# First batch of a fused attention and expert kernel: where the group norm's chain and the next batch's row norm stand in the order by hand

## The reference, cut to what matters

```
def _L0_attn_ref(x, Wqkv_w, Wqkv_b, gn_w, gn_b, out_w, out_b):
    qkv = x @ Wqkv_w.T + Wqkv_b
    a = jnp.einsum('bthd,bshd->bhts', q, k)
    ctx = jnp.einsum('bhts,bshd->bthd', a, v)
    g = ctx.transpose(0, 2, 3, 1)
    mean = g.mean(axis=(2, 3), keepdims=True)
    var = ((g - mean) ** 2).mean(axis=(2, 3), keepdims=True)
    gh = (g - mean) * jax.lax.rsqrt(var + EPS)
    gh = gh * gn_w.reshape(H, Dh, 1) + gn_b.reshape(H, Dh, 1)
    return ctx @ out_w.T + out_b
...
x = x + _layernorm(_L0_attn_ref(_layernorm(x, axis=-1), ...), axis=-1)
x = x + _layernorm(_L0_ffn_ref(_layernorm(x, axis=-1), ...), axis=-1)
```

## Time and profile before

| | us |
|---|---|
| median of 3 runs | 855.06 |
| the 3 runs | 855.31, 852.76, 855.06 |
| the profiled execution | 854.16 |
| its span in the trace | 852.4 |
| PE busy in the span | 784.7 (92%) |
| DVE busy | 583.6 (68%) |
| ACT busy | 487.4 (57%) |
| POOL busy | 290.2 (34%) |

### The profile page before, as it was taken

One profiled execution on the slowest core, in us unless ns is written; L12 is line 12 of the kernel. 1 busy time (PEld: TensorE's weight loads), 2 busy tenths in 40 slices (PEclk: granted clock), 3 DMA queues, 4 the chain that ended last, 5 costly groups with the idle time before them and its releaser, 6 DMA issues.

```text
span 852.4 us, 21050 instructions
## 1 busy us (share of the span) xinstructions
PE 784.7 (92%) x6573; PEld 643.7 (76%) x6582; DVE 583.6 (68%) x1588; ACT 487.4 (57%) x1073; POOL 290.2 (34%) x316
## 2 busy tenths in 40 slices
PE   6989999999999998666999999999999999999991
PEld 2547777777777776444788888888888888888880
DVE  5758989898989888894787444555555555555553
ACT  4355848575766675421566555565656565656562
POOL 3011010101010000072265555555555555555542
PEclk9999999999999999997999999999999999999996
DMA  4114444343526161502244555646464646474733
GB/s 192 50 50 156 119 153 126 141 145 118 162 93 191 64 188 43 149 9 68 48 66 77 100 76 72 125 74 146 75 148 74 145 72 143 71 147 71 145 44 95
DMA packets 102692, 90.10 MB, mean 106 GB/s; under 512 B 63761, under 2 KB 94225, under 8 KB 101457
## 3 DMA queue, kind: packets, MB, share of 16 engines
q1 hardware_dynamic: 87648, 68.45, 27.5%
q0 software_dynamic: 14976, 20.78, 17.1%
HBM read 48.70 MB, written 27.39 MB: 89 GB/s over the span
## 4 chain that ended last, share of the span: by engine, by line
PE 72%; DVE 16%; ACT 5%; issue 4%; POOL 2%; DMA 1%; SPq 0%; ACTq 0%; DVEq 0%; POOLq 0%
PE ps L918 41%; PE ps L933 19%; PE ps L1002 4%; PE ps L1034 3%; DVE wgu L1289 3%; PE ps L996 2%; DVE hf L1229 2%; ACT wgu L778 2%; DVE wdn L1289 1%; DVE st L1405 1%; DVE wdn L1538 1%; PE ps L963 1%; DVE st L1209 1%; DVE hT L1239 1%; PE ps L1005 1%
## 5 line engine op out<-in xcount | busy, mean ns | idle before, releaser
L918 PE MATMUL ps<-xhl,wgu 128*128 128x256 f16 x3102 | 387.6, 275 | 12.3 <-DMA xhl<-attw 6.7
L918 PEld LDWEIGHTS ps<-xhl,wgu 128*128 (+1 forms) x3102 | 304.5, 99 | 56.0 <-issue 8.6
L1229 DVE SCALAR_TENSOR_TENSOR hf<-ps,sc,silu 128x256 f32<-128x256 f32 x330 | 159.6, 484 | 188.8 <-ACT silu L730 163.4
L730 ACT ACTIVATE silu<-ps,sc 128x256 f32<-128x256 f32 x275 | 130.4, 474 | 236.2 <-PE ps L918 236.1
L933 PE MATMUL ps<-wdn,hT 128*128 (+1 forms) x1870 | 252.8, 273 | 9.6 <-DVE hT L1239 7.2
L933 PEld LDWEIGHTS ps<-wdn,hT 128*128 128x128 f16 x1870 | 181.9, 98 | 35.1 <-DVE hT L1239 6.3
L673 POOL DMA_INDIRECT acc_d<-ysb,gst x78 | 128.8, 1651 | 44.5 <-POOL gst L669 30.9
L606 POOL TENSOR_TENSOR rstd<-ve,mhalf 128x4 f32<-128x4 f32 (+1 forms) x32 | 30.7, 960 | 294.6 <-DVE ve L1214 272.9
L1239 DVE TENSOR_TENSOR hT<-hf,hT 128x256 f16<-128x256 f32 x275 | 114.7, 417 | 1.7
L744 ACT CAST hT<-hf 128x256 f16<-128x256 f32 x275 | 109.7, 399 | 8.8 <-DVE hf L1229 7.1
L662 POOL DMA_INDIRECT attw<-xn_d,gst x78 | 80.1, 1027 | 44.5 <-POOL gst L658 32.6
(11 more groups left out here) (245 smaller groups left out, 768.0 us busy)
## 6 DMA issues: line engine op xcount, KB each, us to landing
wgu<-in_gu SPq DMA_DIRECT2D x8, 1408.0 KB, 6.4
att<-in_x SPq DMA_DIRECT2D x16, 512.0 KB, 5.5
wdn<-in_dn SPq DMA_DIRECT2D x8, 768.0 KB, 8.1
x_d<-att SPq DMA_DIRECT2D x8, 512.0 KB, 2.9
xn_d<-wgu SPq DMA_DIRECT2D x8, 512.0 KB, 3.3
acc_d<-ysb SPq DMA_DIRECT2D x16, 256.0 KB, 3.3
att<-x_d SPq DMA_DIRECT2D x8, 512.0 KB, 4.9
att<-acc_d SPq DMA_DIRECT2D x7, 512.0 KB
```

Source lines behind the costliest of these rows:

```text
L730: a.activation(silu[:, c % 2 * TW:(c % 2 + 1) * TW], gu_ps[c % 2][:, 0:TW], ACT.Silu, scale=scale_of(slot, 0)).then_inc(silu_made, 1)
L918: ins = te.matmul(o, slot_gu(slot, hw, k, j), x(hx, k), start=(n == 0), stop=(n == len(TERMS) - 1))
L1229: v.scalar_tensor_tensor(out=hf[lo:P, c % 2 * TW:(c % 2 + 1) * TW], in0=up, scalar=scale_of(slot, 1, lo, P), in1=silu[lo:P, c % 2 * TW:(c ...
```

## The change

Only the table `START` is edited, in batch 0's round. `group_mean` and `group_var` come ahead of `ln1_stats`. `ln1_apply` and `turn1` go from ahead of `ctx_norm` to behind `out`. `prep` 0 comes ahead of `turn1_out`, `prep` 1 stays behind it. PE's filling matmuls are 5, 4 and 10 where they were 9, 9 and 8.

```
-         (0, "ctx_out"), (0, "prep_spread"), (0, "channel_stats"), (0, "busy", 9), (0, "ln1_stats"), (0, "group_mean"), (0, "busy", 9), (0, "group_var"),
-         (0, "busy", 8), (0, "ln1_apply"), (0, "turn1"), (0, "ctx_norm"), (0, "prep_scale"), (0, "turn1_out"), (0, "prep", 0), (0, "prep", 1), (0, "out"),
+         (0, "ctx_out"), (0, "prep_spread"), (0, "channel_stats"), (0, "busy", 5), (0, "group_mean"), (0, "busy", 4), (0, "group_var"), (0, "ln1_stats"),
+         (0, "busy", 10), (0, "ctx_norm"), (0, "prep_scale"), (0, "out"), (0, "ln1_apply"), (0, "turn1"), (0, "prep", 0), (0, "turn1_out"), (0, "prep", 1),
```

## The result

| | before | changed |
|---|---|---|
| median | 854.91 us (5 runs) | 859.26 us (5 runs) |
| lowest, highest | 852.76, 855.31 | 858.46, 860.34 |
| profiled execution, its span | 854.16, 852.4 | 860.27, 858.5 |
| ratio | | 1.0058 (95%: 1.0045 to 1.0072) |

The kernel became 4.35 us slower by the medians, against 5.3 forecast over the profiled execution and a time forecast at 859.5. A second measurement of the same kernel, beside other runs, gave 1.0059 (1.0044 to 1.0073).

The account below looks back on a forecast made before the run. Bound by a chain of waits, mostly over DVE, up to the shared network at 62.26. Profiled 854.16 + 3.95 for later statistics = 858.1, + 1.4 for PE's clock = 859.5 us; 8-in-10 range 856.7 to 862.1.

Parts of the forecast that it names:

- What bounds: Chain of waits from 29 to 62 us, mostly over DVE: losses before 62.26 come out at the end of the run.
- The group norm's chain first: Batch 0's row statistics on DVE start at 33.55 instead of 31.53, 2.0 later; fillers release the variance by a little.
- POOL's order: Group norm's root waits behind the row norm's; two roots take 1.70, so the group norm is applied at 37.33, 1.3 later.
- The projection ahead of the transposes: Transposes, high halves and second weight piece follow the projection; its row statistics start at 47.88 against 43.93, 3.95 later.
- The clock: PE idles 3.6 ahead of the projection; its clock falls to 1.2 GHz and costs 1.4, in full.
- The sum of 3.95: Delay of the projection's row statistics: 1.3 POOL's order, 1.4 the row normalisation now inside, the rest pauses from late transposes.
- The rest at nothing: q keeps 2.4 of cover ahead of k and v; third weight piece, seven fewer fillers, DMAs and SP cost nothing.
- The term of 1.4: Cost of the clock's fall on the projection, taken from 2.85 busy at 0.50 between 382 and 385 us.
- The bound of 3.1: Upper bound on the clock fall's cost, from 48 matmuls at 399.64 taking 8.31 against 5.2.
- The same pause ahead of k and v stays: PE's pause of 2.4 ahead of k and v is the same after the change.
- POOL's root isn't late: Rival: group norm applied at 35.55, 1.8 sooner than summed, PE's pause 1.8 without a fall; 856.3, chance 0.08.
- The clock giving back 4.3 near 382 and 399 us: Rival: the shift lets both low-clock spells end before PE's matmuls, not slower; 853.8, chance 0.07.

Follow-up runs that it names:

- pool_first: Changed kernel, but in batch 0 POOL makes the group norm's root at `group_var`, ahead of the row norm's root; 856.42 us, ratio 1.0025 to the kernel before.
- all_moved: Kernel before with weight pieces split into high and low halves, POOL's roots exchanged, scales ahead of the context, group norm and projection early; 851.64 us, ratio 0.9961.
- filled2: Changed kernel with 25 fillers instead of 10 ahead of the projection and 19 ahead of k and v; 858.67 us, ratio 1.0042 to the kernel before.
- filled: Changed kernel with 25 filling matmuls instead of 10 ahead of the output projection, nothing else; 859.38 us, ratio 1.0062 to the kernel before.
- group_part: Kernel before with only `group_mean` and `group_var` moved ahead of `ln1_stats`, and 18 fillers ahead of the transposes; 856.35 us, ratio 1.0025.
- turn_part: Kernel before with only normalisation, transposes and weight-piece order moved as in the change, `ln1_stats` in front and old fillers; 855.99 us, ratio 1.0025.
- unfilled: Changed kernel without the 10 filling matmuls ahead of the output projection; 859.81 us, against 859.86 for the changed kernel beside it.

## Why the prediction was right, point by point

- **What bounds.** Right: the shift of the statistics from PSUM came out at L918 in the first profile undiminished (6.31 at both), and the span grew by 6.1. From L918 to the end of the span it is 790.1 before and 789.9 after.
- **The group norm's chain first.** Forecast 2.0 later for the row statistics, measured 1.85 (33.38 against 31.53); the variance's matmul started at 32.77. The fillers did not clearly release it, as the forecast had it: its weight load had waited 0.26 for DVE's mean, until 32.69, and the two came within 0.1 us of each other.
- **POOL's order.** L1425 forecast at 37.33, measured 37.20, with a pause of 1.79 that POOL's root ends (1.8 forecast), two roots in 1.68 (1.70). By the Trainium skill, SBUF — State Buffer, on SBUF's two separate sides, a GpSimd operation that reads SBUF and a VectorE operation that is of the fast kind or has two inputs in SBUF exclude each other from a shared pair of ports. The trace agrees: the root of two columns took 0.70 in pool_first and 0.92 beside the normalisation, and the one of four 1.01 alone, 1.71 beside the weight piece of 1.01 and 2.37 beside that of 1.68. In both of these the root ended 0.9 us behind the end of the piece. Beside L1378, which is the same operation with one input from PSUM, the root of all_moved took 1.01.
- **The projection ahead of the transposes.** The chain of 10.55 us from L1425 to the statistics was 47.56 - 37.19 = 10.37 in filled2, where the clock held. The sum of 3.95 was 3.6 there: 0.15 from the group norm's start and 0.2 from the steps behind it.
- **The clock.** That a pause of 3.6 us brings a fall, and that the projection then pays in full, was right; the size was too small. The term of 1.4 measured 2.7 in the first profile (6.7 against 4.00), 1.7 and 2.6 in the two others. By the medians it is less: +4.35 and +5.26 for the changed kernel against +3.48 with both pauses filled, so 0.9 to 1.8, with overlapping intervals. The row of 382 to 385 us had PE busy for 2.85 us at the lower clock; here it was 3.4 to 5.5 us, all of them unbroken matmuls. The bound of 3.1 held. The Trainium skill, TensorE: Matmul & The Clock Gate, Part 1, has it that the lower level is the default and that activity lifts it. The traces agree: all three profiles with a pause of 3.6 showed the fall, two of them within it and one 0.3 us behind it, and those with 0.35 at the same place (filled and filled2) did not.
- **The rest at nothing.** Right for q (2.3 of pause was left ahead of k and v) and for the DMAs. "The same pause ahead of k and v stays" was true, but I did not count that the clock can fall behind it too, though the clock had held there in the kernel before; it did fall in pool_first, group_part and filled, each time for about 1.5 us at L918.
- **The rivals.** "POOL's root isn't late" was forecast at 856.3, and pool_first, which makes it true, had 856.42. There too some luck is in it: that price has no fall of the clock, and the profile had one, of 1.5 us. The clock giving back 4.3 near 382 and 399 us did not happen: from 330 to 420 us the mean granted clock was 0.89 in both kernels.
- **The time.** 859.26 against 859.5 is closer than the terms deserve, and that is luck. The shift of 3.95 was 0.3 too large and the clock's term too small in each profile. The base time lay 0.75 under the median of before, and the shift forecast, 5.3, was 1.0 above the 4.35 of the medians; these two nearly cancel.

**What stays open.** The time from L918 to the end of the span varied between 789.2 and 791.4 over the profiles of all these kernels, which do the same work there. That is as large as the clock's term. The lower clock between 330 and 420 us doesn't explain it: filled2 had the higher mean clock there, 0.92 against 0.89 in the kernel before, and the longest time, 791.4 against 790.1. In filled and filled2 a part of it lies before that, at full clock: ACT's normalisation L838 waited 1.47 and 1.31 us for a DMA (`x_d<-att`; at 259.12 and 175.44), and behind it PE stood for 0.90 and 0.74 ahead of L956, where the profile of the kernel before has no pause. What makes up the rest, and why the runs of one kernel stand up to 4.1 us apart (filled), the runs don't show.

## What to carry to other kernels

Where several engines walk one list of steps, ask for every moved step which engine has its part of the chain at another step: here the root that the moved chain needed stayed behind a root whose input came last, and a wait of 1.8 us took the place of 1.4 us of work. Before work is moved behind a long matmul, follow what it feeds: the transposes fed high halves, these stood in front of a weight piece on ACT, and that in front of the statistics on DVE, which cost 2.1 us. What lay in front of the statistics was work that nobody needed soon, and moving that made the kernel 2.8 us faster, 3.6 with the other moves of all_moved on top.

## What the runs showed of the hardware that I had not expected

- A pause of 3.6 us before the projection brought the clock down to 1.2 GHz in three profiles of three, and it then stayed down through 3.4 to 5.5 us of unbroken matmuls: 1.7 to 2.7 us lost. Behind a pause of 2.3 to 2.5 us ahead of k and v it fell in three profiles (pool_first, filled, group_part) and not in six others (before, the three of the changed kernel, turn_part, unfilled).
- The fall need not lie in the pause. In those three profiles it came 1.0 to 1.1 us after PE had resumed, in the second one of the changed kernel 0.3 us after. Whoever looks only at the clock in the pause finds 1.00.
- The fillers bought nothing here by themselves: with 10 or none of them ahead of the projection the time was the same (859.86 and 859.81), and filling a pause of 2.47 in the kernel before changed nothing that can be measured (1.0007).
- A root of four columns on POOL takes 1.01 alone and 2.37 beside a DVE operation of 1.68: the overlap that the order offered cost 1.4 us on the path. Beside the operation of 1.28 with an input from PSUM (L1378) it takes 1.01 as well.
